# Router and experts in one block, with three semaphores in place of a barrier, and a new order of ScalarE's first steps

## The reference, cut to what matters

```
x = x + 0.5 * ffn(layernorm(x), ...)      # layer 0
x = x + attn(layernorm(x), ...)           # layer 1
x = x + 0.5 * ffn(layernorm(x), ...)      # layer 2

# inside ffn, after its causal attention (16 heads of 8):
h = rmsnorm(x, ln2_w)
probs = softmax(h @ router_w)                      # 8 experts
topv, topi = top_k(probs, 2)                       # 2 experts for each token
topv = topv / sum(topv)
act = silu(h @ w_gate[e]) * (h @ w_up[e]) * weight # 448 hidden columns per expert
x = x + sum over e of act @ w_down[e]
```

## Time and profile before

| what | us |
|---|---|
| median of 3 runs | 1886.57 |
| lowest and highest run | 1883.26, 1888.81 |
| the profiled execution | 1885.49 |
| its span, first to last instruction | 1883.9 |
| router block of layer 0, first to last instruction | 517.7 to 552.7 |
| expert tiles of layer 0, first gather to last scatter | 553.9 to 672.8 |
| router block of layer 2 | 1712.4 to 1747.4 |
| first gather of layer 2 | 1748.5 |

### The profile page before, as it was taken

How to read it: one execution, slowest core, us unless ns; L and a number is a source line. 1 busy time by engine, 2 the same in 40 slices (tenths; PEclk the granted TensorE clock), 3 DMA queues, 4 the chain that set the end, 5 groups by cost and what they waited for, 6 DMA issues and landing times. The chain is left out here.

```text
span 1883.9 us, 31586 instructions
## 1 busy us (share of the span) xinstructions
PE 1660.7 (88%) x11190; PEld 769.4 (41%) x11190; DVE 1377.9 (73%) x2863; ACT 1096.3 (58%) x2301; POOL 445.0 (24%) x492
## 2 busy tenths in 40 slices
PE   4899999999849947899999999478999999994795
PEld 2333333333239933233333332233333333323795
DVE  7888999987153348889999983388899999835333
ACT  2355777677616614356777678234577676782463
POOL 6400201101016737001102020170010010200574
PEclk9788999999959967889999999678899999995898
DMA  4500203300011134200202000242002020001113
GB/s 129 128 14 3 52 3 98 73 2 2 8 33 43 47 100 140 52 2 2 52 2 52 3 2 2 60 140 52 2 2 52 2 52 2 2 2 30 34 48 89
DMA packets 63581, 75.92 MB, mean 40 GB/s; under 512 B 13656, under 2 KB 56221, under 8 KB 62105
## 3 DMA queue, kind: packets, MB, share of 16 engines
q1 hardware_dynamic: 54184, 62.13, 13.1%
q0 software_dynamic: 4992, 9.40, 2.0%
q10 hardware_dynamic: 4224, 2.10, 0.4%
HBM read 53.05 MB, written 21.46 MB: 40 GB/s over the span
## 5 line engine op out<-in xcount | busy, mean ns | idle before, releaser
L751 ACT ACTIVATE probs<-ps 128x512 f32<-128x512 f32 (+3 forms) x1920 | 879.1, 543 | 470.0 <-PE ps L859 468.6
L602 DVE TENSOR_REDUCE mpart<-ps 128x1 f32<-128x512 f32 (+3 forms) x1680 | 1014.7, 666 | 114.3 <-PE ps L813 63.3
L813 PE MATMUL ps<-ka,qa 96*128 96x512 bf16 (+3 forms) x1920 | 670.4, 372 | 35.7 <-DMA ka<-ksplit 22.8
L859 PE MATMUL ps<-qa,ka 96*128 96x512 bf16 (+3 forms) x1920 | 616.4, 357 | 1.4 <-DMA qa<-guard 0.8
L872 PE MATMUL ps<-probs,vv 128*9 128x512 f32 (+3 forms) x3840 | 442.0, 532 | 8.8 <-ACT probs L751 8.1
L700 POOL TENSOR_SCALAR_AFFINE_SELECT probs<-probs 128x512 f32<-128x512 f32 x192 | 121.8, 634 | 1177.3 <-ACT probs L751 1177.3
L813 PEld LDWEIGHTS ps<-ka,qa 96*128 96x128 bf16 x1920 | 192.0, 101 | 479.6 <-DVE mpart L602 339.1
L859 PEld LDWEIGHTS ps<-qa,ka 96*128 96x128 bf16 x1920 | 183.5, 100 | 186.9 <-ACT probs L751 69.1
L816 PE MATMUL ps<-mask_rows,identb 128*128 128x128 bf16 x768 | 161.7, 235 | 0.0
L1207 DVE TENSOR_TENSOR probs<-probs,ps 112x512 f32<-112x512 f32 x78 | 53.7, 688 | 144.3 <-ACT probs L1175 144.3
L1132 PE MATMUL ps<-hT,probs 128*112 128x128 f32 x1248 | 152.5, 277 | 2.9 <-ACT probs L1162 1.8
(11 more groups left out here) (166 smaller groups left out, 962.6 us busy)
## 6 DMA issues: line engine op xcount, KB each, us to landing
qa<-qsplit SPq DMA_DIRECT2D x27, 384.0 KB
ka<-ksplit SPq DMA_DIRECT2D x27, 384.0 KB
probs<-rope SPq DMA_DIRECT2D x12, 512.0 KB, 7.0
qa<-qsplit SPq DMA_DIRECT2D x36, 96.0 KB
ka<-ksplit SPq DMA_DIRECT2D x36, 96.0 KB
qsplit<-arena SPq DMA_DIRECT2D x6, 384.0 KB, 3.0
ksplit<-arena SPq DMA_DIRECT2D x6, 384.0 KB, 2.9
tokens<-arena SPq DMA_DIRECT2D x2, 1024.0 KB, 7.3
```

The lines of the kernel that those rows point to most:

```text
L602: dve.tensor_reduce(mpart[:, j % MD, h0:h0 + some, qt, kc], ps[:, bank, 0:some * w].rearrange("p (h w) -> p h w", h=some), axis=AX.X, op=A ...
L751: act.activation(probs[:, s % 2, h, 0:n], ps[:, u % SB, 0:n], ACT.Exp, scale=SCALE).then_inc(probs_ready, 1)
L813: ins = pe.matmul(dst, qa[0:KROWS, b, h0 + k, tile * 128:(tile + 1) * 128], ka[0:KROWS, b, h0 + k, kc * CH:kc * CH + n], start=True, stop= ...
L859: pe.matmul(dst, ka[0:KROWS, b, h, kt * 128:(kt + 1) * 128], qa[0:KROWS, b, h, c * CH + q0:(c + 1) * CH], start=True, stop=True).then_inc( ...
```

## The change

The block of the router and that of the experts become one, so the barrier between them goes. In its place stand three semaphores, each raised once by VectorE: `experts_found` after `eti`, `rows_found` after `from_row`, and `targets_found` after `to_row`. GpSimd waits for the stored tokens and for `rows_found` before its first gather, and for `targets_found` before its first scatter; ScalarE and TensorE wait for `experts_found`; VectorE waits for `targets_found` before its first `weight`. ScalarE copies experts 0 and 1 first, then does one Silu of a single column of ones into a new tile `table`; and the copy of turned tile 1 stands behind Silu 0.

```diff
-                    dve.tensor_scalar(eti[:, :], etf[:, :], float(E - 1), None, ALU.min)
+                    dve.tensor_scalar(eti[:, :], etf[:, :], float(E - 1), None, ALU.min).then_inc(experts_found, 1)
...
-                    dve.tensor_scalar(from_row[:, :], slot_f[:, 1, :], -1.0, 0.0, ALU.add, ALU.max)
+                    dve.tensor_scalar(from_row[:, :], slot_f[:, 1, :], -1.0, 0.0, ALU.add, ALU.max).then_inc(rows_found, 1)
...
-                    dve.tensor_scalar(to_row[:, :], slot_f[:, 1, :], 0.0, None, ALU.max)
+                    dve.tensor_scalar(to_row[:, :], slot_f[:, 1, :], 0.0, None, ALU.max).then_inc(targets_found, 1)
...
-        with nc.Block() as block:
-
             @block.gpsimd
...
+                    pool.wait_ge(tokens_stored, 32)
+                    pool.wait_ge(rows_found, 1)
                     for u in range(XR - 2):
                         gather(u)
+                    pool.wait_ge(targets_found, 1)
...
                 with pe.If(layer != 1):
+                    pe.wait_ge(experts_found, 1)
                     turn(0)
...
                     act.wait_ge(weights_loaded, 64)
+                    act.wait_ge(experts_found, 1)
                     copy_expert(0)
+                    copy_expert(1)
+                    act.activation(table[:, :], ones[:, 0:1], ACT.Silu)
                     copy_turned(0)
                     for i in range(NSLOT):
-                        if i + 1 < NSLOT:
+                        if 1 <= i and i + 1 < NSLOT:
                             copy_turned(i + 1)
                             copy_expert(i + 1)
                         act.wait_ge(gate_up_ready, 2 * i + 1)
...
                         act.activation(sgb[i % 2], ps[0:MR, 2 * (i % 2), :], ACT.Silu).then_inc(silu_ready, 1)
+                        if i == 0:
+                            copy_turned(1)
...
+                    dve.wait_ge(targets_found, 1)
                     weight(0)
```

More of the change, by code:

```diff
@@ L208, in macaron_kernel @@
     choice = sb("choice", [128, NSLOT, TOPK])
+    table = sb("table", [128, 1])
     slot_w = sb("slot_w", [128, XR + 1])
@@ L323, in macaron_kernel @@
     weight_found = sem("weight_found")
+    rows_found = sem("rows_found")
+    targets_found = sem("targets_found")
+    experts_found = sem("experts_found")
     taken_ready = sem("taken_ready")
```

## The result

The changed kernel took 1882.53 us in the median of 20 runs (1877.66 to 1886.68), the kernel before 1887.01 in 20 runs beside them (1883.26 to 1891.33). The ratio estimated from the runs is 0.997, with a 95% interval from 0.9963 to 0.9978: 4.2 to 7.0 us faster. The medians themselves differ by 4.48 us, 0.24%. So the time is clear of no change by its interval, but by its median it falls short of the 0.3% (1880.9) from which the prediction would call it faster. The forecast was 1880.0 and a saving of 6.45.

What follows compares the result with a forecast made beforehand. A serial chain from router to experts, ahead of a loop at TensorE's rate, was taken as the bound. Gathers 1.35 + 1.30, first tiles 2 x 1.7 and layer 1 0.4 made 6.45 us: forecast 1880.0, range 1876.8 to 1884.1.

Steps and rivals of the forecast that it cites:

- What bounds the kernel there: Router to experts, layers 0 and 2: a serial chain precedes a loop at TensorE's rate, so a lead won there stays.
- The gathers: First gather, layers 0 and 2: without the barrier it starts 1.35 and 1.30 us earlier, after 0.8 us of GpSimd preparation.
- The first tiles: First turn to tile 2, layers 0 and 2: earlier expert copy and Silu 0 save 1.7 us per layer.
- The rival of the stuck gather: First gather waits behind VectorE's halving, taking back 2.0 us per layer: 1884.1 in all; chance 0.09.
- the one in which the barrier wasn't the cause: GpSimd's own start costs the 2.15 us, so the gathers start no earlier: 1882.8; chance 0.09.
- The clock: TensorE's rise to full clock, forecast at no cost; rival: one tile late, 1.5 us per layer, 1883.1; chance 0.17.
- 1881.6 for one late layer: TensorE's clock rises one tile late in one layer instead of two; counted within the late clock's chance of 0.17.
- one of the prediction's own signs of being wrong: TensorE during tile 1: a clock still at 0.50 there was listed among what would show the prediction wrong.
- The prediction's argument that the clock could rise more reliably: After tile 0, TensorE's idle time shrinks by 0.9 us, so the clock could rise more reliably; nothing taken for it.
- Layer 1: Layer 1's two jumps past router and experts: without the barrier the second starts 0.4 us earlier, bounds nothing and 0.9.
- Slower by fetching code: Rival at the router-experts seam: code-fetch pauses in each of three layers cost 14.5 against 6.45 us: 1894.6; chance 0.05.

Runs made afterwards that it cites:

- merged block alone: Changed kernel with ScalarE's first steps in the old order (expert 1 and table load after the turned tiles): 1884.08, ratio 0.9986, beside the kernel before at 1887.39.
- ScalarE's order alone: Kernel before, with its two blocks and barrier, and ScalarE's steps as in the changed kernel: 1885.16, ratio 0.9987, beside the kernel before at 1887.39.
- changed, second execution: The changed kernel itself run again as control on another fast chip: 1883.61 in 12 runs, ratio 0.9986, beside the kernel before at 1887.39.
- changed, pauses filled: Changed kernel plus one unread matmul behind each of TensorE's first three turns: 1882.30 in 12 runs, ratio 0.9964, beside the kernel before at 1888.25.
- changed, clock kept longer: Changed kernel, halvings behind the first weight, unread TensorE matmuls (36, 3 between groups, 18, and 3 behind the first turn): 1879.13 in 6 runs, ratio 0.9956.

## Why the prediction was right, and where its sum was too large

**What bounds the kernel there: right.** The serial chain ahead of the loop set the time, and what was won up to tile 2 (2.96 and 1.48 us) was still there at the last scatter (3.05 and 1.56). On the chip where the loop itself waited it wasn't shown.

That the lead is then kept to the end of the program was taken for granted, and single executions don't show it. This is the start of layer 1's last layernorm in the merged block alone and in ScalarE's order alone.

```profile
1201.29 0.38 DVE L660 BATCH_NORM_AGGREGATE mv<-stats 128x2 f32<-128x6 f32 x4
```

```profile
1197.97 0.38 DVE L657 BATCH_NORM_AGGREGATE mv<-stats 128x2 f32<-128x6 f32 x4
```

| layer 0 (fast chips, one execution each) | last scatter earlier than before | F to layer 1's last layernorm |
|---|---|---|
| before | | 644.63 |
| merged block alone | 1.24 | 644.72 |
| ScalarE's order alone | 1.80 | 644.57 |
| changed | 3.05 | 641.21 |
| changed, second execution | 3.10 | 641.19 |
| changed, pauses filled | 3.01 | 641.24 |
| changed, clock kept longer | 4.85 | 638.46 |

Leads of 1.24 and 1.80 us are gone by then, and one of 3.05 has become 3.42. In both parts alone the clock stayed at 0.50 for 13.65 us at one place of layer 1's attention (from 760.89 and from 757.60), where the kernel before and the changed one have 6.83. So behind the loop a lead is not passed on as it is, and what differs there in the traces is how long the clock stays low; that this is the cause wasn't tried by an experiment. Only the median of many runs tells what a lead is worth, and there the two series of the changed kernel give 4.5 and 3.8.

**The gathers: right, a little too small.** GpSimd's preparation is 0.91 and 0.84 us, against the 0.8 taken from the scatter. The gain at the first turn is 1.57 and 1.61 against 1.35 and 1.30, because the first gather also got shorter, 1.20 and 1.09 instead of 1.65 and 1.58. The prediction had left that length as it was, with up to 0.7 better as a bound. At its old place it began in the middle of the halving; now it begins ahead of it, and takes 1.20 with or without it. Whether the old 1.65 was the halving's doing wasn't tried by itself. By the Trainium skill ("SBUF — State Buffer", section "Who interferes with whom") a VectorE instruction with two inputs in SBUF and a GpSimd instruction that reads SBUF contend, and the second to issue waits until the first is finished. The trace agrees with a wait of that kind for one halving instruction: the second gather beside the halving takes 1.34 and 1.45, and 0.96 with it moved away, where one of the four halving instructions takes some 0.62. No gather waited for all four. The rival of the stuck gather is out, and so is the one in which the barrier wasn't the cause.

**The first tiles: right where the clock let them.** ScalarE's order alone gave 1.6 in each layer, against 1.7. In the changed kernel layer 0 gave 10.38 - 8.99 = 1.39; the missing 0.3 is the low clock. The prediction had named the turns (0.45 instead of 0.30) and not tile 0 (3.72 instead of 3.51); the clock rose at the same time as before while the work came earlier.

**The clock: the step that failed.** The prediction took nothing for it and kept 1.5 per layer as a rival, with 1881.6 for one late layer. That rival is what came, not the forecast's own mechanism in full, and with it one of the prediction's own signs of being wrong: a clock still at 0.50 during tile 1. Its range of 1876.8 to 1884.1 took this in. In layer 2 the rise came when tile 1 was nearly done, at 13.05 instead of 9.63 us from `from_row`, and turn to tile 2 took 10.49 instead of 8.99. The first tiles' gain there was -0.14 instead of 1.7. Two executions of the changed kernel show it in layer 2, and in the merged block alone the clock is as late; with the pauses filled it isn't in the one execution there is, and the loss is gone. The prediction's argument that the clock could rise more reliably, with less idle time after tile 0, didn't hold: with the first turn 1.6 us earlier it rose in layer 2 3.4 us later.

**Layer 1: too large.** 0.4 was taken, 0.04 is seen; six executions of the merged block have 7.93 to 8.52 us for the passage, 8.14 in the mean, and the two with the barrier 8.22 and 8.38, so it may be 0.2, less than the spread. The branch begins earlier and mostly takes longer, 4.99 to 5.59 us against 4.84 to 5.00.

**Slower by fetching code: no.** Nothing like it shows at the seam; where the branch falls through it takes 0.07 us as before.

With the measured terms the sum reads 1.57 + 1.61 for the gathers, 1.39 - 0.14 for the first tiles and 0.04 for layer 1: 4.47 us, against 4.48 between the medians. That they agree so closely is luck: the terms come from one execution of each kernel, the interval of the result is 4.2 to 7.0, and on the second chip the same stretches (3.10 and 1.51 to the last scatter) stand beside 3.78 between the medians. Shown are the terms up to the last scatter and their causes.

## What to carry to other kernels

A serial seam between two loops is worth what its chain measures, and a gain ahead of a loop is still there at the loop's end if the loop goes at one engine's own rate. Behind it, later changes of the clock can take it or add to it, so it is judged by medians. Before such work is moved earlier, look at when TensorE's granted clock rises relative to it: here the rise didn't come along, and a tile that arrived ahead of it took 3.56 us instead of 1.97. Matmuls that nobody reads, put where the engine idles anyway, gave about as much again as the change itself (8.3 us below the kernel before with them and the halving moved, 3.8 without).

## What the hardware showed that was not expected

- Without added matmuls in the router, the rise of the clock came at two moments only, 9.6 to 9.8 or 13.0 us after `from_row`, in all executions but those on the slow chip, which also had 8.4, 15.1 and 16.5. With the first turn at 5.3 to 5.4 us it was the earlier one in both layers; with the turn at 3.7 to 3.9 it was the earlier one in layer 0 and the later one in layer 2, in three executions out of three, until the pauses between the tiles were filled. On the slow chip, too, layer 2 had 13.0 with the early turn (twice) and 9.6 with the late one. What makes layer 2 differ from layer 0 stays open.
- The router's transposes and logits keep TensorE busy for some 10 us and don't raise the clock: in the changed kernel it is still at 0.50 over 530 to 531, with TensorE busy the whole time. This is the window.

```profile
530.00:531.00 1.00, 1.00 (x7) 1.00 (x6) 0.00 (x0) 0.98 (x2) 0.00 (x0) 0.50 1.20 170
```

- From `from_row` of layer 0 to that of layer 2 it took 1194.6 to 1194.8 us in four executions (before, each part alone, and the changed kernel) and 1191.2 to 1191.4 in the other four on fast chips, the changed kernel's second among them; there was nothing between.
- One chip ran every kernel some 34 us slower, with waits of TensorE in the loop over the tiles and the full clock granted. Its cause was not tried.
- The second gather loses 0.4 to 0.5 us beside VectorE's halving in the changed kernel, and the first one, which starts ahead of it, nothing; its 1.20 against 0.96 is its own.
